# Expert choice in head-major order, and the output mix placed behind a P.V run

## The chip, the cores and the metric

The kernel runs on one core of a Trainium2 chip. Its engines work side by side, each from its own queue in order: PE (TensorE, matrix products), DVE (VectorE), ACT (ScalarE), POOL (GpSimd), and SP, which here only starts transfers. The metric is the device time of one execution in microseconds. Before the change it is 2718.7 us, the median of three runs (2717.73 to 2730.42).

## The reference

The input x is 8 batches of 512 tokens of 128 channels, all f32. Six blocks follow one another, each adding to x after a layer norm: a linear layer on inputs rounded block by block to a 6-bit grid, causal attention with one head, the linear layer again, a switch-head attention ("the FFN" below), a Mamba block (a scan over time with 16 states for 256 channels), and the switch-head attention once more. The change touches the switch-head attention alone, which runs 16 times, once per batch and layer:

```
q, k   = x @ Wq[h], x @ Wk[h]                     # 16 heads h of 64
gate_v = einsum('btc,hec->bthe', x, Ws)           # 8 experts e for each token and head
w, sel = top_k(gate_v, 2)                         # the first of equals wins
mix_v  = one-hot of sel, weighted by sigmoid(w)
v      = einsum('bthe,bted->bhtd', mix_v, x @ Wv[e])
attn   = softmax(q k^T / 8) v                     # not causal, 512 x 512 per head
mask_o = one-hot of top_k(x @ Wd, 2)              # experts of the output side
res    = einsum('bthe,bthd,efd->bthf', mask_o, attn, Wo).sum(heads)
```

## The kernel before

**Jobs, slots and steps.** The 16 switch-head attentions are jobs. All engines go through one list of steps, `for g in range(LAST)`, and each issues its share of a step. A job's heads take a slot of 64 steps (`slot(i)`), four per pair of heads and block of query rows: on even steps PE computes two score tiles of 128 x 512 (`scores`, L720), on each step it turns one tile of probabilities in four transposes (`turn_probs`, L729, four steps behind). DVE takes the row maxima of a pair (L1054), ACT the exponentials (L896), and DVE or ACT copies the turned tile out of PSUM (L1297, L1019; while a Mamba block scans it is always ACT).

**Pieces.** Everything else on PE is cut into pieces. The table `PIECES` gives for every kind of work the local step of each piece, `step_of` makes a global step of it, and a sort makes `order`, the one order in which PE issues the pieces. Within a step the sort goes by the piece's name. A piece is called after what it does: `att` (P.V for two heads and 256 rows, L742, 16 matmuls), `back` (turn the attention output of a pair of heads back, L761), `pq` and `pk` (queries and keys, L709), `norm`, `gate` (L776), `value` (L709), `vmix` (mix the experts' values, L789), `omix` (mix the outputs of an eighth of the tokens by the chosen experts, L795, 16 matmuls), `out` (the product with Wo, L802, 32 matmuls), names with `f_` for the first three blocks, with `m_` for Mamba. In PE's own step the turned tile comes first, then the scores, then the step's pieces.

**Two banks.** Piece k writes PSUM bank k modulo 2, and `piece` first waits until piece k - 2 has been taken out (`wait_taken(pe, *order[k - 2][1:])`). ACT takes most pieces, in the step after PE's (`take`, L921 for `att`, L957 for `omix` in two instructions); DVE takes `back` (L1066), `out` (L1094), `f_lin`, `f_att` and `m_out`. So the place of a piece in `order` decides its bank, and which eviction it waits for.

**Three jobs at a time.** While job i runs its heads in a slot, the slot also holds the preparation of job i + 1 ("prep": norm, gates, expert choice, values, their mix) and what comes after job i - 1's heads ("post": the eight `omix` pieces at local steps 16, 20, ... 44, `out` at 47). `att` pieces lie at local steps 10, 14, 18, ..., `back` at 17, 25, ..., so that an `omix` piece stands two steps from the nearest `att`. Beside these run the first three blocks of a later batch and, from the second slot on, a Mamba block per 97 steps.

**Shapes on PE.** `att` multiplies with a stationary 128 x 64 (its two heads go to the two halves of the columns), `omix` too (L795, 64 output rows); scores are 64 x 128, all other pieces and the transposes 128 x 128 (`m_dt` 64 x 128).

**Mixing.** The chosen experts' weights go to DRAM and come back as block-diagonal matrices, so that PE can mix. For outputs: `chosen_o` to `mo_d` (L637), spread to `mo_blocks`, and for each piece a load of `mo_diag` (L528) and one of the attention output `att2` (L456), each issued by SP one step after `omix` piece c - 2.

**Expert choice** (`top2`, L1118 to L1135, on DVE). Gates of 16 heads x 8 experts for 4 x 128 tokens lie as `gates[P, 2, J, E*H]`: experts outside, heads inside (the weights are written that way at the start). Per side a (0: values, 1: outputs) there are two rounds of maximum, compare, times a falling key, maximum, compare; between the rounds the first choice is pushed down. Keys are uint16. The reductions therefore run over a view with the experts innermost, in steps of 16 elements. `mix_gates` (L1145) makes `mix` from sigmoid and picks. `top2` issues one part per step from step 18 (side 0) and from step 45 (side 1) of prep.

## Time and profile before

| | |
|---|---|
| median of 3 runs | 2718.7 us |
| profiled execution | 2719.64 us |
| its span, first to last instruction | 2717.8 us |
| mean granted share of PE's clock | 0.978 |
| busy: PE, DVE, ACT, POOL | 94%, 78%, 68%, 27% of the span |
| `omix`, L795 (2048 matmuls) | 152.2 us busy |
| `att`, L742 (4096 matmuls) | 502.1 us busy |
| `at_d` to `att`/`att2` loads, issue to landing | 3.9 us, median |

Spans of instructions are in us, means of one instruction in ns. A matmul in f32 stands as two instructions. Ends of matmuls are modelled and overlap the next one's start, so the distance of two starts on PE says more than a duration. In a group's row, the part behind the second bar is the idle time of the engine just before these instructions, and what ended it.

### The profile page before, as it was taken

The page shows a single profiled execution, that of the slowest core. Times are in us where ns is not written, and L with a number is a line of the kernel's source. Part 1 is how long each engine was busy: PE and PEld are TensorE (multiplying, and loading weights), DVE is VectorE, ACT ScalarE, POOL GpSimd, SP SyncE. Part 2 cuts the span into 40 slices and gives each one's busy share as a digit, 9 for nine tenths or more (in the row PEclk, how much of TensorE's full clock was granted, in tenths as well). Part 3 has the DMA queues.
Part 4 walks back from the last instruction along what each step waited for, and adds up shares of the span by engine and source line. Part 5 has one row for each costly group of instructions (what it writes and reads, how often), then busy time and mean ns, then how long its engine had stood idle before and what let it go on. Part 6 is the DMA issues. An engine that isn't in the chain of part 4 may idle for free.

```text
span 2717.8 us, 51121 instructions
## 1 busy us (share of the span) xinstructions
PE 2549.3 (94%) x17437; PEld 1694.5 (62%) x17437; DVE 2131.2 (78%) x3103; ACT 1857.1 (68%) x4430; POOL 745.0 (27%) x564
## 2 busy tenths in 40 slices
PE   5699999999999999999899999999999999999996
PEld 3556675665666757566575666656566665766665
DVE  7588776989789898878987998797788878865552
ACT  3365755867688677867776877687687768766663
POOL 1000000544155125603540452164045215500000
PEclk9799999999999999999999999999999999999997
DMA  4525354664566546556573665656476564745424
GB/s 138 139 68 143 94 142 104 162 177 113 143 156 171 137 131 189 141 136 170 137 181 96 186 162 144 161 145 181 107 190 163 142 161 134 197 103 146 122 75 89
DMA packets 753406, 385.77 MB, mean 142 GB/s; under 512 B 421568, under 2 KB 678656, under 8 KB 752768
## 3 DMA queue, kind: packets, MB, share of 16 engines
q1 hardware_dynamic: 747104, 380.66, 53.3%
q8 instruction: 145, 2.38, 0.4%
q10 hardware_dynamic: 6048, 1.84, 0.3%
q14 instruction: 109, 0.89, 0.1%
HBM read 274.91 MB, written 115.87 MB: 144 GB/s over the span
## 4 chain that ended last, share of the span: by engine, by line
PE 63%; DVE 20%; issue 8%; DMA 3%; ACT 2%; POOL 2%; SPq 1%; ACTq 0%; DVEq 0%; POOLq 0%
PE ps L720 13%; PE ps L742 12%; PE ps L729 12%; PE ps L789 7%; PE ps L709 6%; DVE h_ring L1235 5%; PE ps L795 4%; DVE h_nmax L1054 3%; PE ps L802 2%; DVE h_ring L1245 2%; PE ps L761 1%; POOL h_ring L656 1%; DMA v_d<-h_v_mixed 1%; SPq L518 1%; PE ps L829 1%
## 5 line engine op out<-in xcount | busy, mean ns | idle before, releaser
L896 ACT ACTIVATE h_prob<-ps,h_nmax 128x512 f32<-128x512 f32 x1024 | 710.8, 696 | 94.3 <-DVE h_nmax L1054 92.0
L1054 DVE TENSOR_REDUCE h_nmax<-ps 128x2 f32<-128x1024 f32 x512 | 622.1, 1215 | 112.6 <-PE ps L720 112.1
L729 PE MATMUL ps<-ident,h_prob 128*128 128x128 f32 x4096 | 618.5, 278 | 21.2 <-DVE h_probT L1297 13.4
L729 PEld LDWEIGHTS ps<-ident,h_prob 128*128 128x128 f32 x4096 | 477.3, 143 | 190.2 <-issue 107.7
L720 PE MATMUL ps<-h_qk 64*128 64x512 f32 x2048 | 583.4, 646 | 0.6 <-ACT h_prob L896 0.6
L1019 ACT ACTIVATE h_probT<-ps 128x512 f32<-128x512 f32 x796 | 478.6, 601 | 61.3 <-PE ps L729 58.6
L665 POOL TENSOR_TENSOR h_wide_c<-h_wide_c,h_ring 128x512 f32<-128x512 f32 x240 | 336.6, 1402 | 664.9 <-DVE h_ring L1245 664.9
L742 PE MATMUL ps<-h_probT,h_v_sb 128*64 128x256 f32 x4096 | 502.1, 387 | 5.9 <-DMA h_v_sb<-v_d 4.0
L742 PEld LDWEIGHTS ps<-h_probT,h_v_sb 128*64 128x64 f32 x4096 | 273.0, 137 | 312.7 <-issue 148.4
L1235 DVE TENSOR_TENSOR_SCAN h_ring<-h_ring 128x512 f32<-128x512 f32 x256 | 397.7, 1554 | 41.9 <-POOL h_ring L656 23.7
L656 POOL TENSOR_TENSOR h_ring<-h_m_xpad,h_m_b_rows 128x512 f32<-128x512 f32 x256 | 352.7, 1388 | 265.0 <-DVE h_m_xpad L1356 253.2
L789 PEld LDWEIGHTS ps<-h_pv,h_mix_diag 128*128 128x128 f32 x2048 | 256.6, 200 | 63.3 <-issue 51.1
L789 PE MATMUL ps<-h_pv,h_mix_diag 128*128 128x64 f32 x2048 | 266.8, 285 | 28.4 <-DMA h_mix_diag<-mix_blocks 16.5
L1297 DVE COPY h_probT<-ps 128x512 f32<-128x512 f32 x228 | 156.8, 688 | 167.8 <-PE ps L729 167.4
L921 ACT ACTIVATE h_attT<-ps 128x256 f32<-128x256 f32 x256 | 99.0, 387 | 248.1 <-PE ps L742 247.9
L896 ACT ACTIVATION_READ_ACCUMULATOR h_prob<-ps,h_nmax 128x1 f32 x1024 | 219.9, 215 | 0.0
L950 ACT ACTIVATE h_v_mixed<-ps 128x512 f32<-128x512 f32 x128 | 76.7, 599 | 203.4 <-PE ps L789 172.7
L720 PEld LDWEIGHTS ps<-h_qk 64*128 64x128 f32 x2048 | 155.7, 186 | 88.0 <-issue 76.9
L795 PEld LDWEIGHTS ps<-h_mo_diag,h_att 128*64 128x64 f32 x2048 | 134.6, 143 | 100.8 <-issue 47.3
L907 ACT ACTIVATE h_ring<-h_wide_a,A_neg 128x512 f32<-128x512 f32 x256 | 186.4, 728 | 0.4
L1245 DVE TENSOR_TENSOR h_ring<-h_ring,h_m_c_rows 128x512 f32<-128x512 f32 x240 | 177.1, 738 | 2.5
L928 ACT ACTIVATE h_qk<-ps 128x512 f32<-128x512 f32 x256 | 154.2, 602 | 33.4 <-PE ps L709 28.0
(214 smaller groups left out, 2609.2 us busy)
## 6 DMA issues: line engine op xcount, KB each, us to landing
h_mix_diag<-mix_blocks SPq DMA_DIRECT2D x128, 512.0 KB, 4.3
v_d<-h_v_mixed SPq DMA_DIRECT2D x128, 256.0 KB, 4.4
h_v_sb<-v_d SPq DMA_DIRECT2D x128, 256.0 KB, 3.4
at_d<-h_att SPq DMA_DIRECT2D x128, 256.0 KB, 3.1
h_mo_diag<-mo_blocks SPq DMA_DIRECT2D x128, 256.0 KB, 3.5
h_att<-at_d SPq DMA_DIRECT2D x128, 256.0 KB, 3.9
h_m_b_rows<-dbl_d SPq DMA_DIRECT2D x128, 256.0 KB, 4.6
h_m_c_rows<-dbl_d SPq DMA_DIRECT2D x128, 256.0 KB, 4.5
```

The lines of the kernel that those rows point to most:

```text
L656: pool.tensor_tensor(mb["scan"][:, (b * UN + v) % NSC, :], mb["xpad"][:, h, CONV - 1:], mb["b_rows"][:, n % 2, :], ALU.mult).then_inc(sem( ...
L665: pool.tensor_tensor(mb["y"][:, h, :], mb["y"][:, h, :], mb["scan"][:, (b * UN + v) % NSC, :], ALU.add).then_inc(sem("summed"), 1)
L720: ins = pe.matmul(ps[:, SB + 2 * w % 4 + o, :], qk[o * DH:(o + 1) * DH, p % 2, 0, j * P:(j + 1) * P], qk[o * DH:(o + 1) * DH, p % 2, 1, :] ...
L729: ins = pe.transpose(ps[:, TB + v % 2, k * P:(k + 1) * P], prob[:, v % NB, k * P:(k + 1) * P], ident[:, :])
L742: ins = pe.matmul(bank[o * DH:(o + 1) * DH, 0:2 * P], v_sb[:, p % 2, k, o * DH:(o + 1) * DH], probT[:, v % PROBT + o:v % PROBT + 4:2, k * ...
L789: ins = pe.matmul(bank[:, at:at + DH], mix_diag[:, c % 2, g, :, o:H:2], pv2[:, c % 2, g, :], start=True, stop=True)
L795: ins = pe.matmul(bank[0:DH, g * E * TO:(g + 1) * E * TO], att2[:, c % 2, g, :], mo_diag[:, c % 2, g, :, :].rearrange("p t e -> p (t e)"), ...
L896: act.activation(prob[:, v % NB, :], ps[:, SB + v % 4, :], ACT.Exp, bias=nmax[:, p, j, o:o + 1], accum_out=den[:, p, j, o:o + 1]).then_inc ...
L1019: act.activation(probT[:, w % PROBT, :], ps[:, TB + w % 2, :], ACT.Copy).then_inc(sem("probT_act"), 1)
L1054: dve.tensor_reduce(nmax[:, p, j, :], ps[:, SB + 2 * w % 4:SB + 2 * w % 4 + 2, :], X, ALU.max, negate=True).then_inc(sem("row_max"), 1)
L1235: dve.tensor_tensor_scan(place, mb["decay"][:, w % NDC, :], place, 0.0, ALU.mult, ALU.add).then_inc(sem("state"), 1)
L1245: dve.tensor_tensor(mb["y"][:, h, :] if n == 0 else place, place, mb["c_rows"][:, n % 2, :], ALU.mult).then_inc(sem("read"), 1)
```

## The change

The experts now lie inside the heads: gates, keys, picks, sigmoids keep the order of the weights, `(h e)`. The weights' eviction at the start is a plain copy, the key is 8 columns wide and repeated for each head, `g_top` has a tile of its own, and `g_key` and `g_pick` lose their side index. The reductions read eight neighbours; the top and first values are broadcast along the innermost eight. Only `mix` keeps the old order, since DRAM wants it, and is written by four instructions.

In `PIECES`, `omix` moves by two steps (18, 22, ... 46) and `out` to 49, and the sort puts `att` first and `omix` second within a step, everything else behind them in the old order.

```diff
@@ -94,7 +94,7 @@
-        first_key = sb("first_key", [P, E * H], U16)
+        first_key = sb("first_key", [P, E], U16)
@@ -236,7 +236,7 @@
         PIECES = {
             "heads": [(4 * a + 10, "att", a) for a in range(HALF)] + [(8 * p + 17, "back", p) for p in range(PAIRS)]
             + [(8 * p - 5, "pq", p) for p in range(PAIRS)] + [(8 * p - 4, "pk", p) for p in range(PAIRS)],
-            "post": [(16 + 4 * c, "omix", c) for c in range(NCO)] + [(47, "out", 0)],
+            "post": [(18 + 4 * c, "omix", c) for c in range(NCO)] + [(49, "out", 0)],
             "prep": [(11, "norm", 0), (15, "gate", 0), (16, "gate", 1)]
             + [((21, 23, 26, 29)[j], "value", j) for j in range(J)]
             + [((39, 42, 45, 48, 50, 53, 55, 58)[c], "vmix", c) for c in range(NCV)],
@@ -247,7 +247,9 @@
             + [(14, "m_dbl", 0)] + [(17 + c, "m_dt", c) for c in range(HALVES)] + [(MAMBA_STEPS - 1, "m_out", 0)],
         }
         AT = {(what, c): u for pieces in PIECES.values() for u, what, c in pieces}
-        order = sorted((step_of(kind, n, u), what, c, n) for kind, n in BASE for u, what, c in PIECES[kind])
+        FIRST_IN_STEP = {"att": 0, "omix": 1}
+        order = sorted(((step_of(kind, n, u), what, c, n) for kind, n in BASE for u, what, c in PIECES[kind]),
+                       key=lambda piece: (piece[0], FIRST_IN_STEP.get(piece[1], 2), piece[1:]))
         BY_DVE = {"back", "out", "f_lin", "f_att", "m_out"}
 
 
@@ -324,14 +326,13 @@
             nT = t("nT", [P, S])
             nT_split = t("nT_split", [P, 2, 2, S], F32R)
             gates = t("gates", [P, 2, J, H * E])
-            GATES_AT_ONCE = 1
-            g_top = nrm[:, 0, 0:GATES_AT_ONCE * J * H].rearrange("p (n h) -> p n h", h=H)
-            g_first = t("g_first", [P, GATES_AT_ONCE * J, H], U16)
-            g_key = t("g_key", [P, 2, J, E * H], U16)
-            g_pick = t("g_pick", [P, 2, J, E * H], U16)
+            g_top = t("g_top", [P, J * H])
+            g_first = t("g_first", [P, J * H], U16)
+            g_key = t("g_key", [P, J * H, E], U16)
+            g_pick = t("g_pick", [P, J * H, E], U16)
             chosen_o = t("chosen_o", [P, J, H * E])
-            g_sig = t("g_sig", [P, J, E * H])
-            mix = t("mix", [P, J, E * H])
+            g_sig = t("g_sig", [P, J, H * E])
+            mix = t("mix", [P, J, E, H])
             pv = t("pv", [P, 2, E * DH])
             pv2 = t("pv2", [P, 2, VG, DH])
             mix_diag = t("mix_diag", [P, 2, VG, TV, H])
@@ -415,7 +416,7 @@
...
-            turns += [(w_raw[name][:, 0, :], gateT[:, a, :].rearrange("p (e h) -> p e h", h=H)) for a, name in enumerate(("Ws", "Wd"))]
+            turns += [(w_raw["Ws"][:, 0, :], gateT[:, 0, :]), (w_raw["Wd"][:, 0, :], gateT[:, 1, :])]
...
@@ -995,10 +996,7 @@
                                       ).then_inc(sem("weights_qk" if name in ("Wq", "Wk") else "weights"), 16)
                     for n, (_, dst) in enumerate(turns):
                         act.wait_ge(sem("w_turned"), n + 1)
-                        src = ps[:, n % 2, 0:D]
-                        if len(dst.shape) == 3:
-                            src = src.rearrange("p (h e) -> p e h", h=H)
-                        act.activation(dst, src, ACT.Copy).then_inc(sem("w_turned_out"), 1)
+                        act.activation(dst, ps[:, n % 2, 0:D], ACT.Copy).then_inc(sem("w_turned_out"), 1)
                     act.wait_ge(sem("w_turned_out"), len(turns))
                     act.activation(Wve_split[:, 0, :], WveT, ACT.Copy, scale=0.5).then_inc(sem("Wve_hi"), 1)
                     act.activation(WqT[:, 0, :, :], qk_f32[:, 0, :, :], ACT.Copy,
@@ -1101,49 +1099,47 @@
 
                     def top2(i, a, m):
 
-                        n = GATES_AT_ONCE * J
                         r, part = divmod(m, TOP_PARTS)
-                        g, key, pick = (z[:, a:a + GATES_AT_ONCE, :, :].rearrange("p a j (e h) -> p (a j) e h", h=H)
-                                        for z in (gates, g_key, g_pick))
-                        top, first = (z[:, :, :].rearrange("p n (o h) -> p n o h", o=1).broadcast_to([P, n, E, H])
+                        JH = J * H
+                        flat = gates[:, a, :, :].rearrange("p j c -> p (j c)")
+                        g = flat.rearrange("p (n e) -> p n e", e=E)
+                        top, first = (z[:, :].rearrange("p (n a) -> p n a", a=1).broadcast_to([P, JH, E])
                                       for z in (g_top, g_first))
-                        by_expert = first_key[:, :].rearrange("p (n c) -> p n c", n=1).broadcast_to([P, n, E * H])
+                        by_expert = first_key[:, :].rearrange("p (a e) -> p a e", a=1).broadcast_to([P, JH, E])
+                        key, pick = g_key[:, :, :], g_pick[:, :, :]
                         linked()
-                        if m == TOP_PARTS - 1:
-                            link(dve.scalar_tensor_tensor(
-                                out=g.rearrange("p n e h -> p (n e h)"), in0=pick.rearrange("p n e h -> p (n e h)"),
-                                scalar=NEG, in1=g.rearrange("p n e h -> p (n e h)"), op0=ALU.mult, op1=ALU.add))
-                            return
                         if part == 0:
-                            link(dve.tensor_reduce(g_top[:, :, :], g.rearrange("p n e h -> p n h e"), X, ALU.max))
+                            link(dve.tensor_reduce(g_top[:, :], g, X, ALU.max))
                         elif part == 1:
                             link(dve.tensor_tensor(key, g, top, ALU.is_equal))
                         elif part == 2:
-                            flat = key.rearrange("p n e h -> p n (e h)")
-                            link(dve.tensor_tensor(flat, flat, by_expert, ALU.mult))
+                            link(dve.tensor_tensor(key, key, by_expert, ALU.mult))
                         elif part == 3:
-                            link(dve.tensor_reduce(g_first[:, :, :], key.rearrange("p n e h -> p n h e"), X, ALU.max))
+                            link(dve.tensor_reduce(g_first[:, :], key, X, ALU.max))
                         elif part == 4:
                             link(dve.tensor_tensor(pick if r == 0 else key, key, first, ALU.is_equal))
+                        elif r == 0:
+                            link(dve.scalar_tensor_tensor(out=flat, in0=pick.rearrange("p n e -> p (n e)"), scalar=NEG, in1=flat,
+                                                          op0=ALU.mult, op1=ALU.add))
+                        elif a == 0:
+                            dve.tensor_tensor(pick, pick, key, ALU.add).then_inc(sem("chosen_v"), 1)
                         else:
-                            if a == 0:
-                                ins = dve.tensor_tensor(g_pick[:, 0, :, :], g_pick[:, 0, :, :], g_key[:, 0, :, :], ALU.add)
-                                ins.then_inc(sem("chosen_v"), 1)
-                            if a + GATES_AT_ONCE == 2:
-                                if i >= 1:
-                                    dve.wait_ge(sem("mo_out"), 16 * i)
-                                dve.tensor_tensor(chosen_o[:, :, :].rearrange("p j (h e) -> p j e h", e=E),
-                                                  g_pick[:, 1, :, :].rearrange("p j (e h) -> p j e h", h=H),
-                                                  g_key[:, 1, :, :].rearrange("p j (e h) -> p j e h", h=H),
-                                                  ALU.add).then_inc(sem("chosen_o"), 1)
+                            if i >= 1:
+                                dve.wait_ge(sem("mo_out"), 16 * i)
+                            dve.tensor_tensor(chosen_o[:, :, :].rearrange("p j (h e) -> p (j h) e", e=E), pick, key,
+                                              ALU.add).then_inc(sem("chosen_o"), 1)
 
                     def mix_gates(i):
 
                         if i >= 1:
                             dve.wait_ge(sem("mix_out"), 16 * i)
                         dve.wait_ge(sem("chosen_v"), i + 1)
-                        dve.scalar_tensor_tensor(out=mix[:, :, :], in0=g_sig[:, :, :], scalar=1.0, in1=g_pick[:, 0, :, :],
-                                                 op0=ALU.add, op1=ALU.mult).then_inc(sem("mix"), 1)
+                        pick = g_pick[:, :, :].rearrange("p (j h) e -> p j h e", j=J)
+                        for j in range(J):
+                            ins = dve.scalar_tensor_tensor(out=mix[:, j, :, :].rearrange("p e h -> p h e"),
+                                                           in0=g_sig[:, j, :].rearrange("p (h e) -> p h e", e=E), scalar=1.0,
+                                                           in1=pick[:, j], op0=ALU.add, op1=ALU.mult)
+                        ins.then_inc(sem("mix"), 1)
 
                     def split_nT(i):
 
...
```

## Rows read from the trace of the kernel before

**Rows 1.** the page: busy times; the chain that ended last

```profile
PE 2549.3 (94%) x17437; PEld 1694.5 (62%) x17437; DVE 2131.2 (78%) x3103; ACT 1857.1 (68%) x4430; POOL 745.0 (27%) x564
...
PE 63%; DVE 20%; issue 8%; DMA 3%; ACT 2%; POOL 2%; SPq 1%; ACTq 0%; DVEq 0%; POOLq 0%
```

**Rows 2.** PE's waits (total us, times, longest), two groups by line

```profile
PE ps L772 <- DVE nrm L143: 19.4, 8, 3.1
PE ps L709 <- DVE h_att L1066: 13.5, 6, 4.7
PE ps L729 <- DVE h_probT L1297: 13.4, 11, 3.2
...
L789 PE MATMUL ps<-h_pv,h_mix_diag 128*128 128x64 f32 x2048 | 266.8, 285 | 28.4 <-DMA h_mix_diag<-mix_blocks 16.5 <-issue 8.3 <-DVE h_att L1066 3.2
L795 PE MATMUL ps<-h_mo_diag,h_att 128*64 128x64 f32 x2048 | 152.2, 230 | 19.3 <-DMA h_att<-at_d 15.2 <-ACT h_f_big L990 2.1 <-ACT h_qk L928 1.1
```

**Rows 3.** PE's timeline (start, length, us): a step with omix, one without

```profile
1504.91 1.13 PE L720 MATMUL ps<-h_qk 64*128 64x512 f32 x4
1505.97 1.15 PE L795 MATMUL ps<-h_mo_diag,h_att 128*64 128x64 f32 x16
1507.04 0.66 PE L729 MATMUL ps<-ident,h_prob 128*128 128x128 f32 x4
...
2663.89 1.13 PE L720 MATMUL ps<-h_qk 64*128 64x512 f32 x4
2664.95 1.09 PE L729 MATMUL ps<-ident,h_prob 128*128 128x128 f32 x8
```

**Rows 4.** PE's timeline, narrow: att's last pairs, omix's matmuls

```profile
1502.01 0.82 PE L742 MATMUL ps<-h_probT,h_v_sb 128*64 128x256 f32 x6
...
1502.44 0.39 PE L742 MATMUL ps<-h_probT,h_v_sb 128*64 128x256 f32 x2
1502.76 0.33 PE L842 MATMUL ps<-ident,h_f_big 128*128 128x128 f32 x1
...
1506.07 0.40 PE L795 MATMUL ps<-h_mo_diag,h_att 128*64 128x64 f32 x4
...
1506.89 0.22 PE L795 MATMUL ps<-h_mo_diag,h_att 128*64 128x64 f32 x1
```

**Rows 5.** timeline of PE: the last gate matmul and the first of omix

```profile
985.71 0.38 PE L776 MATMUL ps<-gateT,h_nT 128*128 128x256 f32 x1
986.02 0.27 PE L795 MATMUL ps<-h_mo_diag,h_att 128*64 128x64 f32 x1
```

**Rows 6.** timeline of PE: a back piece and the att piece after it

```profile
1507.53 0.60 PE L761 MATMUL ps<-ident,h_attT 128*128 128x128 f32 x4
...
1509.56 1.95 PE L742 MATMUL ps<-h_probT,h_v_sb 128*64 128x256 f32 x16
```

**Rows 7.** groups by line: evictions of back and of att

```profile
L1066 DVE TENSOR_TENSOR h_att<-ps,h_rden 128x512 f32<-128x512 f32 x128 | 88.6, 692 | 44.8 <-PE ps L761 32.1 <-DVE h_rden L1061 0.5
...
L921 ACT ACTIVATE h_attT<-ps 128x256 f32<-128x256 f32 x256 | 99.0, 387 | 248.1 <-PE ps L742 247.9
```

**Rows 8.** DVE's groups by line: expert choice, and nearest shapes

```profile
L1125 DVE TENSOR_REDUCE h_g_first<-h_g_key 128x64 uint16<-128x512 uint16 x64 | 70.0, 1094 | 0.3
L1118 DVE TENSOR_REDUCE nrm<-h_gates 128x64 f32<-128x512 f32 x64 | 65.5, 1023 | 3.5 <-ACT h_g_sig L940 3.3
...
L1135 DVE TENSOR_TENSOR h_chosen_o<-h_g_pick,h_g_key 128x512 f32<-128x512 uint16 x16 | 17.5, 1094 | 0.2
...
L1127 DVE TENSOR_TENSOR h_g_key<-h_g_key,h_g_first 128x512 uint16<-128x512 uint16 x32 | 13.9, 434 | 0.3
...
L1145 DVE SCALAR_TENSOR_TENSOR h_mix<-h_g_sig,h_g_pick 128x512 f32<-128x512 f32 x16 | 12.3, 769 | 0.8
...
L167 DVE TENSOR_REDUCE h_f_sc<-h_f_rows 128x16 f32<-128x512 f32 x12 | 8.2, 681 | 0.2
...
L180 DVE SCALAR_TENSOR_TENSOR h_att<-h_att 128x128 f32<-128x128 f32 x1 | 0.3, 293 | 0.0
```

More of the change, by code:

```diff
@@ L630, in _ @@
                                     sp.dma_start(mix_d.rearrange("(j p) c -> p j c", p=P),
-                                                 mix[:, :, :]
+                                                 mix[:, :, :, :].rearrange("p j e h -> p j (e h)")
                                                  ).then_inc(sem("mix_out"), 16)
@@ L680, in _ @@
                             for e in range(E):
-                                pool.memset(first_key[:, e * H:(e + 1) * H], float(E - e)).then_inc(sem("masks"), 1)
+                                pool.memset(first_key[:, e:e + 1], float(E - e)).then_inc(sem("masks"), 1)
                             for h in range(HALVES):
@@ L1317, in _ @@
                                     wait_taken(dve, "gate", 1, n)
-                                for a in range(0, 2, GATES_AT_ONCE):
+                                for a in range(2):
                                     if TOP_AT[a] <= u < TOP_AT[a] + 2 * TOP_PARTS:
```

## The prediction

> **What bounds the kernel now.** I read the busy shares first: PE is busy 94% of the span, DVE 78%, ACT 68% [rows 1]. A busy share does not say that PE sets the end, so the chain that ended last came next: 63% of it is PE, 8% issue, 20% DVE [rows 1]. PE is first and DVE close behind; an edit that shortens PE pays in some 71% of the span, one that shortens DVE in some 20%. Third, PE's own waits: it stood idle 2717.8 - 2549.3 = 168.5 us, of which 16.5 + 15.2 us for transfers (one wait at the start, and those of the tail) and 19.4 + 13.5 + 13.4 + 3.2 = 49.5 us for DVE results, up to 4.7 us in one piece [rows 2]. The reader is to see there that DVE comes late now and then, by microseconds, and that no single line holds much of PE's idle time.
>
> **Change, part 1: omix behind att.** No instruction is added or removed on PE; 120 of the 128 omix pieces (the last job's eight run in the tail, without P.V runs) move from a step two away into the step of an att piece, directly behind it. What that is worth is read off the starts of PE's groups. *Before:* a step goes scores, omix, next piece: scores to omix is 1.06 us from start to start, omix to the next 1.07; without omix, scores to the next is 1.06 too [rows 3]. So an omix piece costs PE 1.07 us. *After:* att stays where it was, and its way out is replaced. Its pairs of matmuls start 0.22 us apart (0.43 for two), but from the last pair to the next piece, which splits the array otherwise (128*128 behind 128*64), it is 0.32 [rows 4]: 0.10 us is the price of leaving. Omix has the split of att, so I let it start one pair's time behind, at 0.22. Its own way out is the old one. From its second start to its last, 14 steps, there are 0.82 us, 0.059 each [rows 4]; the first step is 0.10, 0.04 to 0.05 longer, since the second weights come late, and I take that as hidden behind att. So omix now costs 0.22 + 1.02 - 0.32 = 0.92 us, 0.15 less than before, and 120 of them 18.0 us. By the written order 29 of the pieces stood behind a 128*128 piece (14 behind the gates) instead of behind the scores, and paid at the entrance too: the last gate matmul, of 256 columns, to omix 0.31 us [rows 5], where 256 columns within one split take 0.22. That is 0.09 x 29 = 2.6 us. Sum: 20.6 us of PE work. Bounds: below, omix finds no better entrance than another piece (2.6), or waits for something new (below). Above, it starts in the idle column half at once: 0.26 us each, 31 us and 2.6.
>
> Not all of it reaches the end. Where the chain runs through DVE, PE only waits longer: 20.6 x 0.71 = 15 us.
>
> **What waits behind the moved pieces.** Each piece takes one of two PSUM banks and waits until the piece two before it has been evicted. In the new order omix stands two behind *back* in 53 cases, and back is evicted by DVE (L1066). From back's start at 1507.53, with some 0.33 to its last matmul, to the modelled end of the next att, 1511.51, there are 3.6 us [rows 6]. The eviction is 0.69 us, but DVE waited for back only 32.1 us in 128 cases, 0.25 each [rows 7]: it mostly comes late. In half of these places value or vmix paid this wait already in the same step; the rows put 13.5 + 3.2 us on it [rows 2], over 49 such places in the old order, 0.34 us a place. For the 27 new ones that would be 9 us. I take 3, since they lie at steps 18 and 34 of a slot, and DVE's two rounds of expert choice begin at 18 and 45. Value or vmix behind omix now waits for att's eviction by ACT (31 places), which is 0.39 us and for which ACT stood waiting 247.9 us in 256 cases [rows 7]; omix takes 0.9 us meanwhile, so it is covered, except where ACT is late: 2 us. Against that stand the waits of omix's old place that go, behind f_turn and pq, 2.1 + 1.1 us [rows 2]. ACT has att's and omix's evictions in one step and none of theirs in the next; softmax and the P copy stand ahead of them in its queue and are not held up. *out* moves behind *back* in its step; att, two behind back there, has out's 32 matmuls in between.
>
> On SP, the two loads that follow an omix (L528, L456) move with it by two steps, past a b_rows or c_rows load at times; their next use stays seven steps away, and POOL, which needs those rows, is busy 27% [rows 1]. The store of x_post moves from step 50 to 52 of a slot; its only near reader is the first Mamba load, at step 54. If the store has not landed by then, SP and the loads behind it wait, once: under 2 us, taken as 0. The tail has no att and stays.
>
> **Change, part 2: experts inside heads.** Per kernel, on DVE [rows 8]:
> - The maximum over 8 experts, read with a step of 16 elements: 1023 ns (f32) and 1094 ns (uint16), 64 each. Read in runs, the nearest row is the quantiser's reduction of 512 elements, 681 ns. It gives 16 results where this gives 64; no row has groups of eight. 64 x (342 + 413) = 48.3 us less (bounds: 0 to that).
> - chosen_o: both sides are now in one order. An instruction of its size without a step takes 692 ns [rows 7]: 16 x (1094 - 692) = 6.4 us less.
> - The compare with the first index, 64 of it at 476 or 434 ns, in the mean 455: the broadcast now lies innermost. L1066, with such a broadcast in f32, takes 692 [rows 7], so 455 to 692. I take the upper end, as the shape is nearest: 15.2 us more; the lower is 0. The f32 compare and the product with first_key (whose rows of eight stay runs) are left as they are.
> - mix: one instruction of 769 ns becomes four of 128 columns that write with a step of 16. 128 columns in runs take 293 ns; the step cost chosen_o 402 ns per 512, so 100 per 128. 4 x 393 = 1572 ns, 16 x 0.80 = 12.8 us more (bounds: 4 x 293, 6.5 us, and twice the step's price, 19 us).
>
> Sum: 54.7 - 28.0 = 26.7 us off DVE's 2131. Of DVE's busy time 0.20 x 2718 / 2131 = 26% lies on the chain, so 7 us reach the end. Bounds: 0, and 26.7 if every saved us meets a waiting PE; with 49.5 us of such waits that is possible.
>
> On the compare, the Trainium skill (Vector Engine (DVE) Microarchitecture Reference, section 5.1, performance modes) says that 2-byte pairs need a step of 1 in every operand, and that one element read over and over as a source of a two-source op ran at the single rate: this speaks against the change and would give the same 15 us; no uint16 row of this trace has such an operand. On mix, section 5.2 of the same page puts a destination stepping 24 words at 2.5 ns per column against 1.05 in runs: 0.19 us for 128 columns, twice the row's 0.10, which by an estimate is 6 us more on DVE and 1.5 at the end.
>
> g_top leaves nrm, and key and pick are shared by the two rounds: DVE alone writes and reads them, in order, so no wait is added. The memsets and weight evictions at the start are as many.
>
> **Sum.** 2719.6 (the profiled execution; span 2717.8) - 15 - 7 + 3 + 2 - 3 = 2699.6. That run is 0.9 us above the median shown, so the median after is 2699, 0.7% less. Under about 0.5% (13.6 us) a measurement of this kernel cannot be told from no change.
>
> **Rivals.** (a) *PE gains, DVE doesn't*: the reductions are bound by their 64 results, not by the step, and compare and mix cost what I say: (28.0 - 6.4) x 0.26 = 5.6 us the other way, 2719.6 - 15 + 5.6 + 2 - 0.9 = 2711; with half the reductions' gain, 2705. For: no row with groups of eight. Against: both reductions are over 340 ns above the one of equal size. (b) *No seam is saved*: omix enters behind att as any piece does; only 2.6 x 0.71 us and DVE's 7 remain: 2719.6 - 1.8 - 7 + 2 - 0.9 = 2712. For: no row has two kinds of piece in one split of columns. Against: leaving a split costs 0.1 us in every row. (c) *Slower: omix as a new door for late evictions.* One bank wait ahead of omix holds the transposes behind it, which DVE and ACT then get late. There are 53 + 31 places; it decides from 22 + 13.6 us over them, 0.42 us at each, and at 0.5, half more than the 0.34 of the old places, it gives 2719.6 - 22 + 42 - 0.9 = 2739. For: the 4.7 us wait [rows 2] is of this kind. Against: 0.34 us is the mean where DVE is latest, and those waits get shorter with part 2. (d) *Both in full*: 2719.6 - 20.6 - 26.7 + 2 - 0.9 = 2673, if DVE's late spots are those of the expert choice.
>
> **Chances.** Forecast 0.52, (a) 0.15, (b) 0.12, (c) 0.10, (d) 0.11. Two thirds of (a) and (b) fall within 0.5%, and a little of the forecast's own spread: faster by over 0.5% 0.69, within 0.5% 0.22, slower 0.09. The range, 2677 to 2716, leaves out (c), half of (d) and the ends of the others.
>
> **What would show it.** In the trace after: att's last pair to omix 0.22 us, omix to the next as before, no scores ahead of omix but in the tail; the reductions at 680 ns, the compares at 690, four mix instructions near 390; PE idle for DVE below 49 us, and of L795 for L1066 under 5. Wrong: omix starts 0.32 behind att's last pair; the reductions stay above 900; L795 waits for L1066 by tens of us.

## Result, and the profile after

The changed kernel took 2701.2 us in the median of 6 runs (2699.2 to 2707.4), the kernel before 2723.7 us in 6 runs beside it (2717.7 to 2730.8): a ratio of 0.9925, 95% interval 0.9909 to 0.9941, 20 us less by the ratio. The forecast was 2699 us. The profiled execution took 2701.69 us, its span is 2699.9, its mean granted clock 0.979 (before: 2719.64, 2717.8, 0.978).

The page of the changed kernel: busy times, and the shares of the chain that ended last.

```profile
PE 2531.9 (94%) x17437; PEld 1703.5 (63%) x17437; DVE 2111.4 (78%) x3151; ACT 1852.6 (69%) x4430; POOL 728.1 (27%) x564
...
PE 67%; DVE 17%; issue 6%; DMA 4%; POOL 2%; SPq 2%; ACT 2%; ACTq 0%; DVEq 0%; POOLq 0%
```

Against [rows 1], PE is busy 17.4 us less and DVE 19.8 us less; the span is 17.9 us shorter. PE's idle time is what it was: 2699.9 - 2531.9 = 168.0 us, before 168.5. PE and issue (time in which an engine waited for nothing that the profile shows) are 73% of the chain instead of 71%, DVE 17% instead of 20%. So between these two traces the whole gain is shorter PE work, and the sum of the waits did not shrink. That is a net result: over all its waits PE stood 65.9 us for DVE before, 61.6 with the new experts alone (experiment 2), 76.5 with the new order alone (experiment 1), and 71.5 with both. Which waits they are has changed. PE's waits after (us in total, times, longest), against [rows 2]:

```profile
PE ps L796 <- DVE h_att L1064: 20.4, 12, 4.4
PE ps L773 <- DVE nrm L143: 18.3, 8, 3.1
PE ps L790 <- DMA h_mix_diag<-mix_blocks: 15.9, 1, 15.9
PE ps L796 <- DMA h_att<-at_d: 15.7, 7, 6.0
PE ps L730 <- DVE h_probT L1293: 15.6, 11, 3.2
PE ps L730 <- ACT h_probT L1017: 10.4, 14, 1.6
```

L796 is omix and L1064 the eviction of back. That wait stood ahead of the value and vmix pieces before, 13.5 + 3.2 us; it now stands ahead of omix, 20.4. Over all of PE's pieces this eviction was waited for 18.6 us before and 22.9 after. (Lines on PE have moved by one: scores L721, turn L730, att L743, back L762, projections L710, vmix L790, omix L796.)

The seam, in a narrow stretch of PE's timeline after (start, length, us): an omix piece from att's last pairs to the next kind of piece. The starts answer to [rows 4].

```profile
1485.76 0.60 PE L743 MATMUL ps<-h_probT,h_v_sb 128*64 128x256 f32 x4
1486.19 0.40 PE L796 MATMUL ps<-h_mo_diag,h_att 128*64 128x64 f32 x4
...
1486.83 0.46 PE L796 MATMUL ps<-h_mo_diag,h_att 128*64 128x64 f32 x5
1487.22 0.33 PE L843 MATMUL ps<-ident,h_f_big 128*128 128x128 f32 x1
```

Att's last two pairs start at 1485.76 and about 1485.98, and omix at 1486.19: 0.43 us for two pairs' time, with no third step of 0.32. Omix's first start to the next piece's is 1.03. In 101 of the 120 pieces the first matmul starts 208 to 210 ns after att's last; the other 19 start 269 ns to 4.8 us after it. On the way out it is 151 to 153 ns in most.

DVE's groups by line after, against [rows 8]:

```profile
L1118 DVE TENSOR_REDUCE h_g_first<-h_g_key 128x64 uint16<-128x512 uint16 x64 | 43.1, 674 | 0.4
L1112 DVE TENSOR_REDUCE h_g_top<-h_gates 128x64 f32<-128x512 f32 x64 | 43.1, 673 | 3.6 <-ACT h_g_sig L941 3.4
...
L1120 DVE TENSOR_TENSOR h_g_pick<-h_g_key,h_g_first 128x512 uint16<-128x512 uint16 x32 | 25.1, 785 | 0.2
...
L1120 DVE TENSOR_TENSOR h_g_key<-h_g_key,h_g_first 128x512 uint16<-128x512 uint16 x32 | 22.3, 696 | 0.3
L1139 DVE SCALAR_TENSOR_TENSOR h_mix<-h_g_sig,h_g_pick 128x128 f32<-128x128 f32 x64 | 19.5, 423 | 0.8
...
L1129 DVE TENSOR_TENSOR h_chosen_o<-h_g_pick,h_g_key 128x512 f32<-128x512 uint16 x16 | 10.9, 684 | 0.2
```

The reductions fell from 1023 and 1094 ns to 673 and 674. The compare with the first index rose to 785 and 696 ns, a mix instruction takes 423. These last three are means with a few long instructions in them: the medians are 681, 680 and 378 ns, and the two compares had 418 and 417 before. The rows that touch the choice add up to some 30 us less, while DVE's busy time fell by only 19.8: neighbours in its queue overlap (added up by the durations of single instructions the rows are 22 us less), and some other rows came out longer, the scans by 3 us.

### The profile page after: what moved, and what is told of

It reads as the page before. It is cut to its first block, busy times and chain, and to the rows that moved or that the text cites. A ratio compares the mean times of both kernels' runs of the same rounds, so it can differ in the third digit from the quotient of the medians.

```text
span 2699.9 us, 51169 instructions
## 1 busy us (share of the span) xinstructions
PE 2531.9 (94%) x17437; PEld 1703.5 (63%) x17437; DVE 2111.4 (78%) x3151; ACT 1852.6 (69%) x4430; POOL 728.1 (27%) x564
## 4 chain that ended last, share of the span: by engine, by line
PE 67%; DVE 17%; issue 6%; DMA 4%; POOL 2%; SPq 2%; ACT 2%; ACTq 0%; DVEq 0%; POOLq 0%
PE ps L721 14%; PE ps L743 12%; PE ps L730 12%; PE ps L790 8%; PE ps L710 7%; DVE h_ring L1231 5%; PE ps L796 4%; DVE h_nmax L1052 3%; PE ps L803 2%; SPq L519 2%; DVE h_ring L1241 2%; DMA h_pv<-pv_d 1%; PE ps L762 1%; POOL h_ring L657 1%; PE ps L808 1%
## 5 line engine op out<-in xcount | busy, mean ns | idle before, releaser
L730 PE MATMUL ps<-ident,h_prob 128*128 128x128 f32 x4096 | 615.4, 278 | 27.7 <-DVE h_probT L1293 15.6
L730 PEld LDWEIGHTS ps<-ident,h_prob 128*128 128x128 f32 x4096 | 477.2, 143 | 207.5 <-issue 119.7
L721 PE MATMUL ps<-h_qk 64*128 64x512 f32 x2048 | 580.7, 644 | 0.1
L743 PE MATMUL ps<-h_probT,h_v_sb 128*64 128x256 f32 x4096 | 501.6, 387 | 6.3 <-DMA h_v_sb<-v_d 3.7
L666 POOL TENSOR_TENSOR h_wide_c<-h_wide_c,h_ring 128x512 f32<-128x512 f32 x240 | 326.5, 1361 | 664.7 <-DVE h_ring L1241 664.7
L743 PEld LDWEIGHTS ps<-h_probT,h_v_sb 128*64 128x64 f32 x4096 | 273.0, 137 | 312.3 <-issue 126.3
L657 POOL TENSOR_TENSOR h_ring<-h_m_xpad,h_m_b_rows 128x512 f32<-128x512 f32 x256 | 345.5, 1359 | 266.4 <-DVE h_m_xpad L1352 247.6
L790 PEld LDWEIGHTS ps<-h_pv,h_mix_diag 128*128 128x128 f32 x2048 | 255.0, 199 | 51.8 <-issue 41.8
L790 PE MATMUL ps<-h_pv,h_mix_diag 128*128 128x64 f32 x2048 | 265.0, 284 | 21.2 <-DMA h_mix_diag<-mix_blocks 15.9
L922 ACT ACTIVATE h_attT<-ps 128x256 f32<-128x256 f32 x256 | 99.4, 388 | 270.1 <-PE ps L743 269.8
L721 PEld LDWEIGHTS ps<-h_qk 64*128 64x128 f32 x2048 | 154.7, 185 | 87.4 <-issue 66.8
L929 ACT ACTIVATE h_qk<-ps 128x512 f32<-128x512 f32 x256 | 155.1, 606 | 47.1 <-PE ps L710 45.8
L796 PEld LDWEIGHTS ps<-h_mo_diag,h_att 128*64 128x64 f32 x2048 | 144.6, 144 | 61.6 <-DVE h_att L1064 27.2
L796 PE MATMUL ps<-h_mo_diag,h_att 128*64 128x64 f32 x2048 | 148.7, 229 | 36.8 <-DVE h_att L1064 20.4
```

Of the source, the lines that this page charges most:

```text
L657: pool.tensor_tensor(mb["scan"][:, (b * UN + v) % NSC, :], mb["xpad"][:, h, CONV - 1:], mb["b_rows"][:, n % 2, :], ALU.mult).then_inc(sem( ...
L666: pool.tensor_tensor(mb["y"][:, h, :], mb["y"][:, h, :], mb["scan"][:, (b * UN + v) % NSC, :], ALU.add).then_inc(sem("summed"), 1)
L721: ins = pe.matmul(ps[:, SB + 2 * w % 4 + o, :], qk[o * DH:(o + 1) * DH, p % 2, 0, j * P:(j + 1) * P], qk[o * DH:(o + 1) * DH, p % 2, 1, :] ...
L730: ins = pe.transpose(ps[:, TB + v % 2, k * P:(k + 1) * P], prob[:, v % NB, k * P:(k + 1) * P], ident[:, :])
L743: ins = pe.matmul(bank[o * DH:(o + 1) * DH, 0:2 * P], v_sb[:, p % 2, k, o * DH:(o + 1) * DH], probT[:, v % PROBT + o:v % PROBT + 4:2, k * ...
L790: ins = pe.matmul(bank[:, at:at + DH], mix_diag[:, c % 2, g, :, o:H:2], pv2[:, c % 2, g, :], start=True, stop=True)
```

## Where a wait for back's eviction comes from

The longest of omix's waits shows what DVE does meanwhile. It is new at omix alone: in the trace of before the value piece of the same place waited 4.70 us for the same eviction (at 1344 us). PE's timeline, changed kernel, 1319 to 1338 us (in brackets the idle time before, and what ended it):

```profile
1319.17 0.60 PE L762 MATMUL ps<-ident,h_attT 128*128 128x128 f32 x4
...
1322.71 1.95 PE L743 MATMUL ps<-h_probT,h_v_sb 128*64 128x256 f32 x16
1329.05 1.97 PE L796 MATMUL ps<-h_mo_diag,h_att 128*64 128x64 f32 x16 [4.38 <-DVE h_att L1064]
1330.94 1.65 PE L710 MATMUL ps<-Wve_split,h_nT_split 128*128 128x512 f32 x3
...
1337.00 0.95 PE L710 MATMUL ps<-Wve_split,h_nT_split 128*128 128x512 f32 x3
```

DVE's timeline in the same stretch:

```profile
1319.28 2.11 DVE L1231 TENSOR_TENSOR_SCAN h_ring<-h_ring 128x512 f32<-128x512 f32 x1
1321.31 0.65 DVE L1112 TENSOR_REDUCE h_g_top<-h_gates 128x64 f32<-128x512 f32 x1
1322.00 0.69 DVE L180 SCALAR_TENSOR_TENSOR h_f_big<-h_f_big 128x512 f32<-128x512 f32 x1
...
1324.01 1.22 DVE L1052 TENSOR_REDUCE h_nmax<-ps 128x2 f32<-128x1024 f32 x1
1325.14 0.90 DVE L1114 TENSOR_TENSOR h_g_key<-h_gates,h_g_top 128x512 uint16<-128x512 f32 x1
1325.97 2.11 DVE L1231 TENSOR_TENSOR_SCAN h_ring<-h_ring 128x512 f32<-128x512 f32 x1
1328.00 0.17 DVE L1059 RECIPROCAL h_rden<-h_den 128x8 f32<-128x8 f32 x1
1328.30 0.69 DVE L1064 TENSOR_TENSOR h_att<-ps,h_rden 128x512 f32<-128x512 f32 x1
```

Back's last matmul starts by 1319.5, its eviction at 1328.30, 8.8 us later. DVE idles for 0.13 us at most in between: Mamba scans, quantiser steps, expert choice and row maxima stand ahead in its written order. The place is step 26 of the slot, inside the first round of expert choice. The prediction gave it the 3.6 us up to the end of the next att. Second, behind the wait the pieces themselves are longer: omix 1.97 us where it takes 1.15, the projection 1.65 and later 0.95. PE's windows there (stretch, its length, busy, granted clock, DMA share, GB/s):

```profile
1300.00:1324.00 24.00, 21.26 (x152) 1.00 0.52 143
1324.00:1329.00 5.00, 0.66 (x8) 0.81 0.00 0
1329.00:1333.00 4.00, 3.95 (x22) 0.50 0.46 118
1333.00:1337.00 4.00, 4.00 (x21) 0.89 0.94 262
1337.00:1341.00 4.00, 4.00 (x30) 1.00 0.09 32
```

PE idled 4.38 us and then worked at 0.50 of its clock, 1.2 GHz, for the 4 us from 1329. A late DVE instruction is paid twice.

## Experiments

The theory T: the two parts act apart; the order is worth PE's seams, 0.15 us each, for which the chain's PE share of 0.71 holds, less a few us of waits; the experts are worth their DVE time by DVE's share. Rivals: F, the order brings its 20.6 us in full but for a few us of new waits; S, no seam is saved and the gain is chance in DVE's timing; B, the new wait for back's eviction takes much of it and can be moved away. Each kernel ran 6 to 12 times. The table gives the ratio to the kernel before that ran beside it, the us that this ratio is, and, for the last section, the time at equal clock (explained there).

| kernel | ratio (95%) | us | at clock 0.976 |
|---|---|---|---|
| before (82 runs) | | | 2723.8 |
| changed (12 runs in two sets) | 0.9925 (0.9909 to 0.9941), 0.993 (0.9905 to 0.9954) | -20, -19 | 2705.8, 2707.4 |
| 1 order alone | 0.9961 (0.9943 to 0.9979) | -11 | 2710.9 |
| 2 experts alone | 0.9969 (0.9954 to 0.9985) | -8 | 2715.9 |
| 3 omix ahead of att | 0.9949 (0.993 to 0.9969) | -14 | 2709.4 |
| 4 omix a step behind att | 1.0021 (1.0007 to 1.0035) | +6 | 2737.4 |
| 5 back a step earlier | 1.0009 (0.9993 to 1.0025) | +2 | 2724.4 |
| 6 a reduction doubled | 1.002 (1.0 to 1.004) | +5 | 2722.3 |
| 7 half the choice | 0.9854 (0.9827 to 0.988) | -40 | 2693.3 |
| 7b the same again | 0.9866 (0.9846 to 0.9885) | -37 | 2692.7 |
| 8 half the choice, old order | 0.9899 (0.9879 to 0.992) | -28 | 2705.5 |
| 9 two omix pieces at once | 0.9977 (0.9961 to 0.9993) | -6 | 2718.1 |
| 10 the same, old choice | 0.9991 (0.9978 to 1.0003) | -2 | 2723.2 |

**1, the order alone**, on the kernel before:

```
-  "post": [(16 + 4 * c, "omix", c) for c in range(NCO)] + [(47, "out", 0)],
+  "post": [(18 + 4 * c, "omix", c) for c in range(NCO)] + [(49, "out", 0)],
...
+  FIRST_IN_STEP = {"att": 0, "omix": 1}     # and the sort by it
```

> The kernel before with the new order alone (omix at 18 + 4c, out at 49, att and omix first in their step); the expert choice stays as it was. As predicted, with PE's saving landing only where PE is on the chain: 20.6 x 0.71 = 15 us, less 2 for new waits, so 13 us less than before. Rival F, PE's saving lands in full and new waits for DVE take a few us back: 17 to 19 us less. On PE both expect att's last pair to omix 0.22 us, and PE idle for DVE at omix (L795 behind L1066) of over 15 us if the late evictions simply move their waiter there.

**2, the experts alone**: the changed kernel without these lines.

> The changed kernel with the old order: only the expert choice is new. As predicted, 26% of the DVE time saved lies on the chain: 5 to 7 us less than before. Rival F: DVE's saving only makes DVE wait longer for PE, within 2 us of before; PE's idle time for DVE stays within 3 us of the 49.5 us of before.

The order is worth 0.39%, the experts 0.31%; 0.9961 x 0.9969 = 0.9930, the whole 0.9925. The parts are additive within the intervals. F would have put the order at 17 to 19 us less; it is 11, by the interval 6 to 16. The experts' 8 us (4 to 13) are more than F's 2. In experiment 1 PE's waits for DVE were (us in total, times, longest; L797 is omix there, L1068 back's eviction):

```profile
PE ps L797 <- DVE h_att L1068: 21.9, 12, 4.7
PE ps L774 <- DVE nrm L143: 19.4, 8, 3.1
PE ps L731 <- DVE h_probT L1299: 17.2, 11, 3.6
```

All three are as long as before or longer. Over all its waits PE stood 76.5 us for DVE here, and 65.9 before; for back's eviction alone 24.6, and 18.6 before. The shorter PE work turned partly into waiting.

**3, omix ahead of att** in the same step, on the changed kernel: `FIRST_IN_STEP = {"omix": 0, "att": 1}`. The seam between the two is kept, only its order turns.

> The changed kernel with omix ahead of att in the same step instead of behind it. If the gain is one change of the array's split saved per omix (scores, omix, att, next: still one entrance and one exit for the two), PE's work is that of the changed kernel, and the time is within 6 us of it, rather above, since omix now asks for back's eviction 1.9 us sooner. If the gain needs omix behind a P.V run (its weights loaded under it), it is lost at least in part: 10 us or more above the changed kernel.

By the ratios it took 5 to 7 us more than the changed kernel, with 7 us of room either way, so the loss itself is not clear of noise. PE was busy 2535.7 us, between the 2531.9 and 2542.9 of the changed kernel's two traces: the saved seam does not need omix to stand behind att. The wait for back's eviction in its trace is now at att (L743), which comes 1 us sooner than omix did (the expectation had omix ask, and 1.9 us sooner):

```profile
PE ps L743 <- DVE h_att L1064: 32.4, 18, 4.5
```

That is 12 us more than at omix after; over all of PE it is 34.1 against 22.9. The sooner after back the second bank is asked for, the longer the wait.

**4, omix in the step behind att**: `19 + 4 * c` for `18 + 4 * c`. All else stays, and S says that nothing should be lost.

> The changed kernel with omix one step later, behind the turned tile of the next step instead of behind att. If splits cost what the starts say, each omix pays 0.15 us more and some 0.09 more at the entrance from a 128*128 piece: 120 x 0.24 = 29 us above the changed kernel, some 10 above the kernel before, less up to 8 us if the waits for back's eviction go. If the gain came from the room between pieces and their evictions instead, it stays within 5 us of the changed kernel.

By the ratios it took 25 to 26 us more than the changed kernel, and PE was busy 2566.1 us, 34 and 23 more than in the changed kernel's two traces. S falls: the seams are real PE time. Two stretches of its timeline, a turned tile and a projection without omix between them, and with it:

```profile
1496.73 0.60 PE L730 MATMUL ps<-ident,h_prob 128*128 128x128 f32 x4
1497.09 0.95 PE L710 MATMUL ps<-Wve_split,h_nT_split 128*128 128x512 f32 x3
...
1501.83 0.60 PE L730 MATMUL ps<-ident,h_prob 128*128 128x128 f32 x4
1502.36 1.15 PE L796 MATMUL ps<-h_mo_diag,h_att 128*64 128x64 f32 x16
1503.43 0.96 PE L710 MATMUL ps<-Wve_split,h_nT_split 128*128 128x512 f32 x3
```

From turn to projection it is 0.36 us without omix and 1.60 with it, so that omix costs 1.24 us there; behind att it costs 0.92. The difference is 0.32, more than the 0.24 that was expected, and PE's waits for DVE are 62.3 us instead of 71.5.

The cleanest view of the seams is the last slot with heads, where no Mamba block runs and PE never waits for more than 0.15 us between its first scores and its last. From the first scores matmul to the last it takes 119.1 us in all three traces with the old order (before, experiments 2 and 8), 117.8 or 117.9 in all nine with omix in att's step (changed twice, experiments 1, 3, 6, 7, 7b, 9, 10), and 120.5 in experiment 4.

**5, back one step earlier**: `8 * p + 16` for `8 * p + 17`, so that its eviction has a step more before omix asks for the bank. B expects a gain.

> The changed kernel with every back piece one step earlier (8p + 16 instead of 8p + 17), so that DVE is asked to evict it a step before the att and omix of 8p + 18. If the new waits of omix for back's eviction (20.4 us in 12 waits) come from the short distance, they fall to under 10 us and the kernel gains 6 to 12 us on the changed one. If DVE is simply behind with everything, the waits turn up at the transposes instead (L730 behind DVE's copies or the exponentials) and the gain is under 3 us.

A miss, and with the wrong sign: 22 us slower than the changed kernel that ran beside it. PE's waits in its trace:

```profile
PE ps L730 <- ACT h_probT L1017: 13.3, 21, 1.8
...
PE ps L777 <- DVE h_att L1064: 8.9, 5, 2.8
PE ps L743 <- DVE h_att L1064: 8.5, 9, 1.9
PE ps L803 <- DVE h_att L1064: 8.0, 5, 2.8
```

The wait left omix and went to the gates (L777), att (L743) and out (L803), 25.4 us in these rows and 30.1 over all of PE, against 22.0 in the changed kernel beside it. The odd step was also left without a piece, so that two turned tiles follow each other in 219 places instead of 120, and 20 of the 21 waits for ACT in the first row stand at the second of two turns. Here the bank wait was not removed by moving the piece that is evicted; it went to other pieces and grew.

**6, one reduction doubled** (part 0 of both rounds issues it twice, 43 us more on DVE), and **7, half the choice**:

```
+  link(dve.tensor_reduce(g_top[:, :], g, X, ALU.max))          # 6: ahead of the same line
...
-  if TOP_AT[a] <= u < TOP_AT[a] + 2 * TOP_PARTS:
+  if TOP_AT[a] <= u < TOP_AT[a] + 2 * TOP_PARTS and not 6 <= u - TOP_AT[a] < 10:   # 7
```

> The changed kernel with the first reduction of each round of expert choice done twice (same result): 64 x 0.67 = 43 us more on DVE, nothing else. If a quarter to a third of DVE's time in the expert choice reaches the end, 11 to 14 us more than the changed kernel. If DVE's part of the change did nothing and its 8 us in the experts-only kernel are an accident of placement, within 4 us.

> The changed kernel with the second round's maximum, compare, key and index steps left out on both sides (the second expert is not searched, the results differ): 32 x (673 + 748 + 484 + 674 ns) = 83 us less on DVE. With the same quarter to third, 21 to 27 us less than the changed kernel; if PE's waits for DVE (71 us in all, much of it not behind the expert choice) run out as DVE gets lighter, 10 to 15 us. PE's waits for DVE fall by about as much as the time.

> The changed kernel itself, as the measure for the three beside it on the same chip: 0.9925 of the time before, within 0.002.

Against the changed kernel beside them, 43 us more DVE time cost 24.5 us, 0.57 each; 76 us less (2036.1 busy against 2112.5) brought 21, 0.27 each. Each of the two times has some 9 us of room, so that 0.57 and 0.27 differ by little more than the noise. The experts' part lies between: 18 us of DVE's busy time (2131.2 before, 2113.0 in experiment 2) for 8 us, 0.46. So DVE's time seems to have no fixed price here: what was added cost more than what was saved brought. The wait for back's eviction follows DVE's load; the two rows are of 6 and of 7:

```profile
PE ps L796 <- DVE h_att L1064: 26.5, 13, 5.1
```

```profile
PE ps L796 <- DVE h_att L1064: 9.7, 9, 2.2
```

**8, half the choice in the old order, and 7b.** If DVE's lateness eats the other half of the seams' worth, the order should bring nearly 20 us where DVE is light.

> The new expert choice with the second round's four search steps left out (results differ), in the old order: the partner of the half-choice kernel in the new order, both with 83 us less on DVE. If the part of omix's 20.6 us that did not arrive (10 of them, with the full choice) was lost to DVE, it arrives here: 17 to 21 us between the two. If it is lost to something that DVE's load does not change (PSUM banks, ACT, the clock), the two differ by 8 to 12 us again.

> The half-choice kernel in the new order once more, for the comparison on the same chip: 0.985 of the time before, within 0.003.

The order brought 9 to 11 us there (ratios, and medians 2696.3 to 2685.6), as much as in experiment 1; the ratios leave some 8 us of room either way, so 17 is just outside. A lighter DVE did not bring out the rest. PE's waits for DVE rise with the order even so, from 50.4 to 58.4 us (57.7 in experiment 7).

**9 and 10, two omix pieces behind every second att**: `22 + 8 * (c // 2)`, on the changed kernel and on experiment 1. This leaves the number of changes of the split as it was in those kernels, since att enters and leaves it in any case.

> The changed kernel with the eight omix pieces in pairs behind every second att (steps 22, 30, 38, 46, both pieces of a pair there), so that none stands two behind a back piece; their seam with att is kept. If the wait for back's eviction is a cost of the place (20 us in 11 or 12 waits), it goes, no other piece takes it over, and the kernel is 8 to 15 us faster than the changed one, near 0.989 of before. If DVE is behind anyway and the wait moves to other pieces, as with back one step earlier, it is within 4 us of the changed one. If five evictions in one step are too much for ACT, slower by 5 us or more, with L710 and L730 waiting for L958.

> The same pairs on the kernel before, with the old expert choice. Order alone in the place of the change gave 10.6 us of the 20.6 of PE work. If the rest went into waits behind back's late eviction, this one has 16 to 20 us less than before; if not, again 9 to 12 us.

Both missed. 9 was meant to beat the changed kernel and is 13 to 14 us behind it (of the three cases that were laid out the third came true in size, but the new wait stands at L796 for L922); 10 brought 2 to 3 us. The two pieces fill both banks at once. From 9's trace, the waits of the projection that comes next and of omix's second piece:

```profile
PE ps L710 <- DVE h_att L1064: 13.8, 8, 4.2
...
PE ps L796 <- ACT h_attT L922: 6.3, 12, 1.4
```

The wait for back moved once more, to the projection; over all of PE it is 16.9 us, less than before. In its place came waits for ACT, 51.1 us over all of PE for 39.9 and 41.4 in the changed kernel's two traces: a second omix asks at once for the bank that ACT has just been given with att. That is part of the loss. Against the changed kernel's second trace, which ran at the same mean clock of 0.973, the span is 15.3 us longer, half of it idle time of PE (174.6 us for 167.0) and half busy time (2550.6 for 2542.9); what the busy half is stays open. No kernel tried was faster than the changed one with all its work.

## Why the prediction was right

By its own steps:

- *Omix 0.92 us instead of 1.07.* Shown. Its entrance is one pair's time, its exit the old one. In the last slot with heads it is 1.2 us for eight pieces, which is 8 x 0.15, and the step between omix's first two matmuls fell from 0.107 to 0.056 us in most of them, as was assumed. PE's busy time fell by 17.4 us where 20.6 were expected; with experiment 2 against the changed kernel it is 24.0. Single profiles of one kernel differ by 11 us in it (2531.9 and 2542.9), since their clocks differ (0.979 and 0.973). Times the mean clock, PE's busy time is 2492 and 2493 us in the traces of experiment 2 and of before, and 2474 to 2479 in the changed kernel's two and experiment 1: 13 to 19 us less.
- *Times 0.71, less 2 net of waits: 13 us for the order.* Measured 11 alone, 11 to 12 on top of the experts, 9 to 11 with a light DVE. The net is right, and that the seams are PE time is held by experiment 4 and the last slot. The factor 0.71 itself was not tested: PE work of 13 to 19 us that arrived in full, less the 7 to 11 us by which PE's waits for DVE grew, would give about the same.
- *New waits behind back's eviction: 3 us, L795 under 5.* This was the mis-sized term, and the sign named with it was wrong for a reason of its own. What is new is the difference over all of PE: 18.6 to 24.6 us in experiment 1, 15.9 to 22.9 or 22.0 from experiment 2 to the changed kernel, 6 to 7 us, twice the term. By places: of the 20.4 us at omix, 15.5 stand at step 26 of the slot, in seven pieces, where the value pieces had waited 13.5 us before. The prediction said that value or vmix paid there already, and did not carry it over into its sign: these waits have only changed the line that they stand at. The new places, steps 18 and 34, hold 4.9 us (4.2 in experiment 1). So the guess that DVE is less late there was nearly right, and the 9 us of the old places' mean would have been too much. Step 26 itself rose by 4 us, to 15.5 in the changed kernel (11.4 in experiment 2) and to 17.6 in experiment 1 (13.5 before), while the vmix pieces at step 58 lost 2 to 3 us of their waits. Why step 26 rose is open.
- *Old waits of omix gone, 3 us.* Their lines (L990 and L928, now L991 and L929) do not stand ahead of omix any more. Over all of PE the waits for ACT went from 41.6 to 40.9 us in experiment 1, but from 37.1 to 39.9 from experiment 2 to the changed kernel; the net of 3 gone and 2 new is too small to be read.
- *DVE 26.7 us less, 7 at the end.* Measured 18 to 20 us of busy time (before to experiment 2, before to changed, experiment 10 to 9; 25 to 27 if experiment 1, whose DVE is 7 us busier than before's, stands for the old choice), and 8.4 at the end (4 to 13 by the interval): less on DVE than forecast, and more of it arrived than the 0.26. The reductions did what the shape of the quantiser's rows said. The compare took its upper end (medians 681 and 680 ns for 692; a few long ones lift the means to 785 and 696). The Trainium skill (Vector Engine (DVE) Microarchitecture Reference, section 5.1) puts such an operand at the single rate, and the rows agree. Mix was taken too dear: of the 64 instructions the median took 378 ns, near my 393, and the mean of 423 comes from three above 1.2 us; but four in a row start some 220 ns apart, so that 14 of the 16 groups span 1.01 to 1.06 us where the sum has 1.57. The step of 16 thus costs 85 ns in the median for 128 columns, below the 100 that the row gave. By an estimate from the Trainium skill's figures (section 5.2 of the same page, 2.5 against 1.05 ns per column for a step of 24 words) it would have been 190; the trace does not bear that out for this step.
- *PE idle for DVE under 49 us.* Wrong in the three rows that made up most of it: they are now 20.4 + 18.3 + 15.6 = 54.3 us. Over all of PE, the prediction's 49.5 us were 65.9, and they became 71.5.

Rival (a), no gain in DVE, falls to the rows of the reductions and to experiment 2; (b), no seam, to experiment 4 and the last slot; (d), both in full, to experiments 1 and 8. Rival (c) names a mechanism that is real and too small to turn the sign: 6 to 7 us are new, where it needed 22. Each part alone came within 3 us of its own forecast (order 11 for 13, experts 8 for 7), and the two misses have opposite signs. That the whole came out at 20 us for 20 is in part luck: the waits were mis-sized by 3 us, DVE's saving by 7, and the measured ratios have some 4 us of room either way.

Left open: how much of the order's PE work is lost, and to what. PE's waits for DVE grew with the order in every pair of traces: 65.9 to 76.5 us, 61.6 to 71.5, and with half the choice 50.4 to 58.4. That is of the size of what is missing from the 20.6, but PE's idle time as a whole did not grow with it in each pair (168.5 to 169.5 us from before to experiment 1). ACT's evictions, the loads from memory and the clock are other candidates, and no run took one of them away. Nor did a run move `out` alone, which went from step 47 to 49 with omix.

## What to carry to other kernels

Put pieces that split PE's array alike side by side, and read the price of a seam from the distances of starts, not from durations. As a first estimate, count only the chain's share of that engine as gained; here that came out, though the factor was not tested by itself. Then list for the new order which bank each moved piece asks for and when the engine that must free it gets there by its own written order; moving the piece again (experiments 3, 5 and 9) moved that wait, and none of the three was faster for it.

## What the runs showed of the hardware

**PE's waits go with a lower clock, and the clock goes with the time.** Within one kernel, run by run, the time falls as the mean granted clock rises: over 198 runs of 12 kernels, each less its kernel's mean, 2.0 us for each 0.001 of clock, correlation -0.77. Of its first six runs the changed kernel took 2699 to 2702 us in four, at 0.979, and 2707 in two, at 0.975. If PE's 2532 us of work were all on the path, 0.001 would be 2.6 us; it is three quarters of that, close to PE's share of the chain. Where the clock goes is seen at 1329 us: 0.50 behind a wait. Between 150 and 2660 us the changed kernel's trace has nine stretches at 0.50, each beginning during a wait of PE of 1.5 to 4.4 us or within 2 us behind it; four waits of 2.2 to 3.2 us have none. The Trainium skill (TensorE: Matmul & The Clock Gate, Part 1) says that the gate follows PE's own activity; the trace agrees, by the 0.50 behind the wait of 4.38 us.

This bears on the table's last column, which moves each kernel's mean by that 2.0 us to the clock 0.976 (standard errors 0.3 to 1.7 us). There, the order alone is 12.9 us (12.8 with half the choice, 8 to 10 on top of the experts) and the experts alone 7.9. The doubled reduction ran at 0.9724 in the mean, and at equal clock it costs 15 us, not 24.5; the halved choice ran at 0.980 and gains 13 to 14, not 21. A good third of what DVE's load does to this kernel seems to go through PE's clock. The adjustment is a correlation: no run set the clock by itself, and a run with longer waits would show both a longer time and a lower clock. Experiment 4 points the same way from the other side: PE is slower but waits less, and it ran at 0.979.

**The price of a change of split**, f32, one matmul record to the next at full clock: 0.10 us on leaving 128*64 for 128*128 (310 ns behind att's 256 columns, where the next pair starts after 209), none between two kinds of matmul within 128*64 (208 to 210 ns from att to omix in 101 of 120 places, the others later).
